# Layer norm with X split in two parts for centring, variance products in four column groups, and the deviations made in four groups of four chunks

## The reference

```python
def _layernorm(x, axis=-1, eps=1e-5):
    m = jnp.mean(x, axis=axis, keepdims=True)
    v = jnp.var(x, axis=axis, keepdims=True)
    return (x - m) / jnp.sqrt(v + eps)
```

## Time and profile before

| | us |
|---|---|
| median of 3 runs (3243.49 to 3248.74) | 3245.59 |
| the profiled execution | 3241.03 |
| its span | 3239.2 |
| norm `l0`, first matmul to last product, about 533.9 to 585.5 | 51.6 |
| norm `la`, 904.9 to 946.3 | 41.4 |
| norm `sp`, 1062.3 to 1105.3 | 43.0 |
| norm `ca`, 2333.5 to 2378.8 | 45.3 |
| norm `ex`, 2993.4 to 3034.6 | 41.2 |

### The profile page before, as it was taken

How to read it: one execution, slowest core, us unless ns; L and a number is a source line. 1 busy time by engine, 2 the same in 40 slices (tenths; PEclk the granted TensorE clock), 3 DMA queues, 4 the chain that set the end, 5 groups by cost and what they waited for, 6 DMA issues and landing times. The chain is left out here.

```text
span 3239.2 us, 61546 instructions
## 1 busy us (share of the span) xinstructions
PE 2933.7 (91%) x23047; PEld 2363.8 (73%) x23047; DVE 1932.0 (60%) x3801; ACT 1415.1 (44%) x3058; POOL 1055.0 (33%) x1104
## 2 busy tenths in 40 slices
PE   6999998588883789999999999999879998999799
PEld 4777776233351549999988999898868887888555
DVE  5556584667734336666666666665247776776465
ACT  2555555111132415555555555554036665666200
POOL 3445452177713015555555555553000000000000
PEclk9999999799987899999999999999589999999799
DMA  7988861000003133344343443442100000000000
GB/s 177 191 180 189 172 162 49 13 1 1 1 3 114 67 107 85 81 88 89 79 89 81 86 89 79 87 86 56 59 6 1 1 1 1 1 1 1 8 23 30
DMA packets 419407, 213.43 MB, mean 66 GB/s; under 512 B 326260, under 2 KB 398604, under 8 KB 417324
## 3 DMA queue, kind: packets, MB, share of 16 engines
q1 hardware_dynamic: 401248, 199.32, 27.4%
q10 hardware_dynamic: 17868, 10.19, 1.4%
HBM read 177.82 MB, written 52.89 MB: 71 GB/s over the span
## 5 line engine op out<-in xcount | busy, mean ns | idle before, releaser
L1698 DVE TENSOR_TENSOR sl_vl_slot<-sl_psV_slot,sl_vh_slot 128x512 fp32r<-128x512 f32 x1024 | 636.1, 684 | 380.8 <-ACT sl_vh_slot L1680 378.7
L1680 ACT ACTIVATE sl_vh_slot<-sl_psV_slot 128x512 fp32r<-128x512 f32 x1024 | 529.5, 605 | 512.1 <-PE sl_psV_slot L1635 511.3
L1653 PE MATMUL sl_psY_slot<-sl_vl_slot,sp_Mh_sp 64*128 64x512 f32 x2048 | 437.3, 390 | 0.8 <-DVE sl_vl_slot L1698 0.3
L1653 PE MATMUL sl_psY_slot<-sl_vh_slot,sp_Mh_sp 64*128 64x512 f32 x2048 | 434.9, 387 | 0.0
L1653 PE MATMUL sl_psY_slot<-sl_vh_slot,sp_Ml_sp 64*128 64x512 f32 x2048 | 434.6, 387 | 0.0
L1611 POOL TENSOR_TENSOR sl_fl_slot<-sl_f_slot,sl_fh_slot 128x512 fp32r<-128x512 f32 x256 | 336.7, 1315 | 20.5
L1609 POOL CAST sl_fh_slot<-sl_f_slot 128x512 fp32r<-128x512 f32 x256 | 166.7, 651 | 451.8 <-PE sl_psV_slot L1635 450.4
L2057 DVE TENSOR_TENSOR ca_ptl_ca<-ca_psT_ca,ca_pth_ca 128x512 fp32r<-128x512 f32 (+1 forms) x272 | 183.9, 676 | 167.3 <-ACT ca_pth_ca L1994 167.3
L1653 PEld LDWEIGHTS sl_psY_slot<-sl_vl_slot,sp_Mh_sp 64*128 64x128 f32 x2048 | 227.2, 184 | 25.8 <-issue 12.6
L1994 ACT ACTIVATE ca_pth_ca<-ca_psT_ca 128x512 fp32r<-128x512 f32 (+1 forms) x272 | 158.9, 584 | 182.3 <-PE ca_psO_ca L87 178.8
L1653 PEld LDWEIGHTS sl_psY_slot<-sl_vh_slot,sp_Mh_sp 64*128 64x128 f32 x2048 | 227.3, 185 | 12.6
(11 more groups left out here) (396 smaller groups left out, 6245.7 us busy)
## 6 DMA issues: line engine op xcount, KB each, us to landing
sl_f_slot<-filt_hat SPq DMA_DIRECT2D x1024, 64.0 KB, 2.2
na_v_na<-na_windows SPq DMA_DIRECT2D x128, 390.0 KB
na_windows<-na_values SPq DMA_DIRECT2D x160, 113.8 KB, 6.8
na_values<-na_vo_na ACTq DMA_DIRECT2D x32, 260.0 KB, 6.9
u_hat<-fw_o_fwd SPq DMA_DIRECT2D x8, 1024.0 KB, 3.8
sl_u_slot<-u_hat SPq DMA_DIRECT2D x128, 64.0 KB, 2.2
y_hat<-sl_y_slot SPq DMA_DIRECT2D x128, 64.0 KB, 1.8
X<-in_x SPq DMA_DIRECT2D x8, 512.0 KB, 7.8
```

What stands on the lines that cost most here:

```text
L1653: mm = e.matmul(psY[half][:, :], left[pl][rows, :], right[pr][rows], start=kc == 0 and k == 0 and x == 0 and z == 0, stop=kc == KC - 1 and ...
L1680: e.activation(v_out(0, n, q), bank(4 * n + q), ACT.Copy).then_inc(S["v_high"], 1)
L1698: e.tensor_tensor(v_out(1, n, q), bank(m), v_out(0, n, q), ALU.subtract).then_inc(S["v_split"], 1)
```

## The change

All of it is in `layer_norm_channels` and the constants that it uses.

- Centring. GpSimd rounds each chunk to fp32r (`x_high`), and x minus that is the low part. The low part is made by VectorE for the chunks in `low_by_vector` and by GpSimd for the others. C(c) becomes two fp32r products with `centre_r`: low part, then high part. The parts have four buffers, so the rounding of chunk c waits for C(c-4).
- Variance. The four products of V(c) go to four groups of 32 columns of the array, with a stationary side of 32 columns, and position block j of the chunk goes to partitions 32j and on. A bank now gathers 4 chunks, and two banks take turns.
- Deviations. Square root, reciprocal, rounding and the low rest are done four times, for 4 chunks each, on all 128 partitions. The rest and the high rows are put together by one `scalar_tensor_tensor` with a per-partition factor `second`.
- S(c) follows V(c+6) instead of V(c+10).
- At the start of the program VectorE makes `centre_r`, `second`, a smaller `mean_row` and a `pick_row` of 64 columns.

```diff
@@ neighbourhood_attention, VectorE, start of the program
-                e.memset(T["mean_row"][:, 0:127], 0.0)
-                e.memset(T["mean_row"][:, 128:255], 0.0)
-                e.memset(T["mean_row"][:, 127:128], 1.0 / C)
+                e.memset(T["mean_row"][:, :], 0.0).then_inc(S["mean_zero"], 1)
                 e.tensor_scalar(T["centre"][:, :], T["ident"][:, :], 1.0 / C, None, ALU.subtract)
-                e.tensor_tensor(T["pick_row"][:, :], T["ident"][:, 0:rows], T["ident"][:, rows:2 * rows], ALU.add)
+                e.tensor_scalar(T["centre_r"][:, :], T["ident"][:, :], 1.0 / C, None, ALU.subtract)
+                e.wait_ge(S["mean_zero"], 1)
+                for at in (15, 31):
+                    e.memset(T["mean_row"][:, at:at + 1], 1.0 / C)
+                halves = T["ident"][:, :].rearrange("p (j z c) -> p z c j", j=TPC, z=2)
+                e.tensor_tensor(T["pick_row"][:, :].rearrange("p (c j) -> p c j", j=TPC), halves[:, 0, :, :], halves[:, 1, :, :], ALU.add)
+                e.tensor_reduce(T["second"][:, :], halves[:, 1, :, :], AX.XY, ALU.add).then_inc(S["mean_zero"], 1)
+                e.wait_ge(S["mean_zero"], 2)
+                e.tensor_scalar(T["second"][:, :], T["second"][:, :], -1.0, None, ALU.mult)
@@ layer_norm_channels
+    NC2, GC, NX = B * NCH, 4, 4
+    NG, LAG = NC2 // GC, 6
+    low_by_vector = (0, 1, 2, 3, 4) if affine else (0, 1, 2, 3, 4, 5, 6, 9, 12)
...
+        def low_part(e, c):
+            e.wait_ge(S["x_high"], c + 1)
+            return e.tensor_tensor(parts[1][c % NX][:, :], img(c), parts[0][c % NX][:, :], ALU.subtract)
...
+            @block.gpsimd
+            def _(e):
+                for c in range(NC2):
+                    if c >= NX:
+                        e.wait_ge(S["c_in_psum"], c - NX + 1)
+                    e.tensor_copy(parts[0][c % NX][:, :], img(c)).then_inc(S["x_high"], 1)
+                    if c not in low_by_vector:
+                        low_part(e, c).then_inc(S["low_by_pool"], 1)
...
                 def centre(c):
...
-                    e.matmul(psC[c % 3][:, :], T["centre"][:, :], img(c), start=True, stop=True)\
+                    if c in low_by_vector:
+                        e.wait_ge(S["low_by_dve"], count(c))
+                    else:
+                        e.wait_ge(S["low_by_pool"], c + 1 - count(c))
+                    e.matmul(psC[c % 3][:, :], T["centre_r"][:, :], parts[1][c % NX][:, :], start=True, stop=False)
+                    e.matmul(psC[c % 3][:, :], T["centre_r"][:, :], parts[0][c % NX][:, :], start=False, stop=True)\
                         .then_inc(S["c_in_psum"], 1)
                 def variance(c):
...
-                        mm = e.matmul(psV[b][:, :], T["mean_row"][:, 127 - t:255 - t], sq[c % 3][:, j * 128:(j + 1) * 128],
-                                      start=(t == 0), stop=(t == NT - 1))
+                        mm = e.matmul(psV[q % 2][32 * j:32 * (j + 1), :], T["mean_row"][:, 15 - c:47 - c],
+                                      sq[c % 3][:, j * 128:(j + 1) * 128], start=(at == 0), stop=(at == GC - 1))
...
-                    if c >= NCH + 2:
-                        spread(c - NCH - 2)
-                for c in range(NCH - 2, NC2):
+                    if c >= LAG:
+                        spread(c - LAG)
+                for c in range(NC2 - LAG, NC2):
                     spread(c)
...
             @block.scalar
...
+                    if c >= GC and c % GC == 0:
+                        deviation(c // GC - 1)
+                deviation(NG - 1)
...
             @block.vector
...
+                for c in low_by_vector:
+                    if c < 7:
+                        low(c)
+                for q in range(NG):
+                    deviation_rows(q)
+                    if not affine and q in (0, 1):
+                        low((9, 12)[q])
+                    for c in range(q * GC, (q + 1) * GC):
+                        scale(c)
```

More of the change, by code:

```diff
@@ L717, in layer_norm_channels @@
         sq = [sb(f"ln_sq{i}", [128, CH]) for i in range(3)]
-        sd = [sb(f"ln_sd{b}", [NT, 128]) for b in range(B)]
-        rstd = [sb(f"ln_rstd{b}", [NT, 128]) for b in range(B)]
-        rows = [sb(f"ln_rows{b}", [128, 128], F32R) for b in range(B)]
+        sd, rstd = ([sb(f"ln_{n}{q}", [128, 128]) for q in range(NG)] for n in ("sd", "rstd"))
+        high, rows = ([sb(f"ln_{n}{q}", [128, 128], F32R) for q in range(NG)] for n in ("high", "rows"))
         zg = [sb(f"ln_zg{i}", [128, CH]) for i in range(2)] if affine else None
@@ L751, in spread @@
                     for j in range(TPC):
[L752 removed]
+                        t = c * TPC + j
                         mm = e.matmul(psR[c % 3][:, j * 128:(j + 1) * 128],
[L754 removed]
+                                      T["pick_row"][:, t:t + 1].to_broadcast([128, 128]), rows[c // GC][:, :],
                                       start=True, stop=True)
@@ new lines, in low, with deviation_rows @@
+                def low(c):
+                    low_part(e, c).then_inc(S["low_by_dve"], 1)
+                def deviation_rows(q):
+                    e.wait_ge(S["sd_done"], q + 1)
+                    e.reciprocal(rstd[q][:, :], sd[q][:, :]).then_inc(S["rstd_done"], 1)
+                    e.wait_ge(S["rstd_done"], q + 1)
+                    e.tensor_copy(high[q][:, :], rstd[q][:, :]).then_inc(S["rows_high"], 1)
+                    e.wait_ge(S["rows_high"], q + 1)
+                    e.scalar_tensor_tensor(rows[q][:, :], high[q][:, :], T["second"][:, 0:1], rstd[q][:, :], ALU.mult, ALU.add)\
+                        .then_inc(S["rows_done"], 1)
```

76 lines of the change are left out of this document (30 added, 46 removed).

## The result

The changed kernel takes 3272.83 us (median of 7 runs, 3259.80 to 3276.09) against 3246.90 of the kernel before (7 runs, 3241.79 to 3250.25) on the same chip. The ratio is 1.0077, with a 95% interval of 1.0065 to 1.0090: 25 us slower. The profiled execution took 3270.96, its span is 3269.2.

The account below looks back on a forecast made before the run. TensorE bounds each norm's first 30 us, then its pause for VectorE's rows ends the high clock. Norms 4 x 40.4 + 49 = 210.6 against 222.5, with the program start -11.1: forecast 3235 us, range 3206 to 3258.

Parts of the forecast that it names:

- the slower rival: Low clock from each norm's first step to its last: 48.9 us a norm, 52.9 for l0, total 3272; chance 0.12.
- (1): Norm start: GpSimd's cast 0.65 and VectorE's rest 0.69 stand ahead of C(0), which starts at 1.5 us.
- (2): Up to S(3), TensorE does 12 C, 10 V and 4 S in 11.8 us.
- (3): At chunk 4, V(5) waits behind ScalarE's table load, 1.9 us with smaller waits; S(3) ends at 15.2.
- (4): TensorE stands 3.1 us ahead of C(12) for VectorE's product and second-group rows, until 18.3; the clock falls.
- (5): After the pause, four steps of C, V, S at the low clock: 9.8 us, to 28.1.
- (6): S(8) waits for the third group's rows and two hand-overs, to 30.5 us.
- (8): The fourth group's deviation rows take 2.4 us, to 37.1.
- (9): Norm end: four S in 3.4 us and the last product in 0.9, to 41.4.
- the contention as a rival: GpSimd 15% slower as VectorE reads the same SBUF chunks: 11.7 us over the five norms, total 3246; chance 0.20.
- Between 34.2 and 41.4 I take 40.4: Length of a norm without affine, between high clock throughout (34.2 us) and low clock after the pause (41.4).
- the high-clock rival: Clock stays high past the pause ahead of C(12): norms of 34.2 us, l0 44.3, total 3205; chance 0.18.

Follow-up runs that it names:

- groups: The changed kernel without the split of X (no casts or low parts, C one fp32 product): 14 us faster than the kernel before, ratio 0.9956.
- parts_unread: The changed kernel with all casts, low parts and waits, but C computed from X as one fp32 product: 24 us slower than the kernel before, ratio 1.0074.
- dense8: after8 with one more unread fp32r product of 512 columns in each C: 15 us faster than the kernel before, ratio 0.9955.
- after8: The changed kernel with deviations for 8 chunks, S(c) behind V(c+10), low parts of chunks 9 and 12 first: 8 us faster than the kernel before, ratio 0.9974.
- split: The kernel before with the split of X alone (casts, low parts, C as two fp32r products): 13 us faster than the kernel before, ratio 0.9959.
- fill: The changed kernel with unread 128x128 fp32r products in three TensorE pauses of the four norms without affine: 19 us slower than the kernel before, ratio 1.0058.

## Why the prediction was wrong, by its own steps

The likeliest case, 3235, failed; the time is next to the 3272 of the slower rival, to which I gave 0.12, and above the range, which ended at 3258. The norms are 32.0 of the 41 us that the profiled execution is over (3271 against 3230): 5.2, 6.6, 5.1 and 9.6 in la, sp, ca and ex, 5.5 in l0. The other 9 are outside the norms, where the forecast had 0.8 for the start of the program, which took 0.66; the rest is not explained.

**The step that failed** is the price of what TensorE waits for. VectorE's operations stood in the sum as if GpSimd were idle (low part 0.61, rows 1.55), and measured 1.02 and 2.6 beside it; the new wait ahead of C(0) stood there as 1.5 us, and not as a pause that ends the clock; and the clock was held to be 1.00 up to the pause ahead of C(12), which la and ca bear out from their first V's on and sp and ex do not. So the 6.6 us a norm that the split takes off TensorE came back as waits and as low clock.

| step, la from its first cast | forecast | measured |
|---|---|---|
| (1) first C | 1.5 | 1.8 |
| (2) first V starts | 2.9 | 4.9 |
| (3) S(3) ends | 15.2 | 17.6 |
| (4) C(12) starts | 18.3 | 21.6 |
| (5) four steps done | 28.1 | 31.9 |
| (6) S(8) starts | 30.5 | 34.5 |
| (8) S(12) starts | 37.1 | 41.2 |
| (9) end | 41.4 | 45.6 |

- Steps (5) to (9), the low clock behind the pause, took 24.0 us against 23.1. That the pause ends the clock, and what the clock then costs, was right in la and ca: a step is 2.59 in place of 2.46 (C 1.10 for 0.855, V 0.58 for 0.75).
- Steps (1) to (4) were mis-sized, by 3.3 us in la: 0.3 at the start; 1.8 in the first three C, 1.02 apart as the low parts come and not 0.46; the pause 0.9. The rest from the first V to S(3) is only 0.3 over: C and V take 1.02 in place of 0.91, and the wait ahead of V(5), for which the forecast had 1.9 with smaller ones, is 0.29. The price of C and V left out that C's products come 0.33 apart next to V, not 0.23 as in the earlier trace rows. The deviation rows were kept at 1.55; beside GpSimd they are 2.6 here. I had the contention as a rival, and put it on GpSimd alone: VectorE's operations between SBUF and SBUF stretch too, L818 from 0.23 to 1.03, L820 from 0.35 to 1.38, and L831 of l0 from 0.75 to 1.67. L818 above starts at 933.38 in the midst of a rest of GpSimd (933.06, 1.26 long) and ends at 934.41, 0.09 behind it: it doesn't share, it waits for the whole of the other's instruction. The Trainium skill, SBUF — State Buffer, SBUF: two separate sides, says just this of VectorE's operations with two inputs in SBUF or in a two-port mode: whichever engine starts first holds the shared ports for its whole instruction. By that rule, the trace agrees, also in that products from PSUM and the reciprocal (0.94 in both places) don't stretch. The prediction left it out.
- "Between 34.2 and 41.4 I take 40.4": behind the pause ahead of C(12) the clock did not come back in any of the four norms, and in sp and ex it fell earlier, at the 10th C. The rival of the low clock throughout was right in the time, and partly luck: its first half came true, every norm begins at 0.50; its second did not, C and V lifted the clock in each of them. Its 48.9 a norm is near that of ex, not of la. In la and ca the high clock was back by C(3) and V(1), in sp and ex only by V(2), and only these two fell at the 10th C. That the late return shifts VectorE's rows into a rest of GpSimd would explain it; no run tests that.
- The reading under it, that a pause of 2.5 us ends the high clock, was not true of every pause in the kernel before: ahead of ex TensorE stood 2.50 too, and its first three C came at the high clock.
- l0, forecast 49, took 54.5. Four L831 at 0.92 or more above their row and two groups of rows at 1.0 more are 5.7 us on VectorE, which is the path there.
- The start of the program was 0.66, forecast 0.8. The column groups work: V is 0.36 to the next C, and groups gains by it.
- The base of the mistake is in the sum itself: it counted what TensorE no longer has to do as saved, and its waits as a thing of their own. parts_unread shows that 6.6 us a norm more of TensorE's work is free in the changed kernel; dense8, with 3.7 more, is no slower than after8, and its profiled norms are shorter. That the pauses act through the clock was known from the earlier trace rows; that less work makes every small wait count was weighed only against the high-clock rival.

The Trainium skill, TensorE: Matmul & The Clock Gate, A second HAM failure mode, stood behind the rival of the low clock throughout: little idling between groups of matmuls, often enough. By that rule, the trace agrees in after8, where waits of 0.24, 0.85 and 0.59 us come ahead of the fall. It doesn't tell why the same steps stay at the low clock in la and leave it in sp.

What stays open: how the 38 us between groups and parts_unread divide over the pause ahead of C(12) (2.98 in la), the start (in la the first C comes 1.7 us later, and the first V another 1.6, at a low clock that groups doesn't have there), the second stretch of low clock and the smaller waits; what decides whether the clock comes back; and whether split could win in full with GpSimd's work ordered around VectorE's rows.

## What to carry to other kernels

- Before halving the work of TensorE, look at how its waits stand to its work afterwards. If other engines feed it piece by piece, the saved columns may come back as a low clock; the same change is good where TensorE stays the bound. Test each half by itself: here both gained 13 to 14 us and together lost 25.
- A wait of TensorE ahead of a long run of small products is worth filling with products that nobody reads: five of them, 1.38 us in a pause of 1.4, took 4.6 us off the profiled norms (and 8 off the time, where the intervals still overlap). It has to be done ahead of the fall: in fill, ex, fillers behind it made the norm longer.
- Price an operation of VectorE between SBUF and SBUF from a row in which GpSimd is at work, or add up to the length of one instruction of GpSimd (here 1.3 us) to it, and the other way round.
- A new wait ahead of a stage's first product adds to the pause between the stages. Read from the trace how long TensorE stood there before (here 1.57 and 2.50 us ahead of la and ex), and at which clock the stage began.
